# A state-space block with layer norm and tensor-train FFN on eight cores: ten state-sum matmuls issued ahead of the normalisation transposes

## Chip, cores, metric

The kernel runs on all 8 cores of one Trainium2 chip. Each core takes 2 of the 16 sequences and works alone; nothing is exchanged. The metric is the device time of the slowest core in microseconds.

## The reference

x is 16 sequences x 2048 steps x 1024 channels. The output is x plus a selective scan plus a linear layer, both on the normalised x:

```python
xn = _layernorm(x, axis=-1)
x = x + attn(xn) + ffn(xn)
# attn:
x_and_res = x @ in_proj_w.T + in_proj_b
x_in = silu(x_and_res[..., :d_model]); res = x_and_res[..., d_model:]
ssm = x_in @ x_proj_w.T + x_proj_b            # 16 + 1024 + 1024 columns
delta = clip(softplus(ssm[..., :16] @ dt_proj_w.T + dt_proj_b), 1e-5, 0.1)
def step(h, inp):                              # h: batch, 1024, 16
    dt, Bt, Ct, xt = inp
    dA = clip(exp(A * dt[..., None]), 1e-6, 1.0)
    h = clip(h * dA + (Bt * dt * xt)[..., None], -100.0, 100.0)
    return h, sum(h, axis=-1) * Ct + D_param * xt
# scanned over the steps; then y * silu(res) @ out_proj_w.T + out_proj_b
```

The FFN is a 1024 x 1024 matrix built from small tensor-train factors.

## The kernel before

**Work.** The two sequences of a core are cut into 8 chunks of 512 steps (TC). A chunk passes through three stages, and the program goes through windows w = 0 to 9 in which three chunks are in work at once: chunk w-2 has its output projection (cO), chunk w-1 its scan (cS), chunk w its normalisation and projections (cP).

**Scan.** A chunk has 8 channel blocks k of 128 x 16 states n, so 128 scans; scan j is block j // 16, state j % 16. For each, ACT computes a decay plane (emit_da, L899, "da j", ring of DAR = 8 tiles), DVE runs one TENSOR_TENSOR_SCAN over 512 steps (L839, "scan j") into the ring h_buf of HR = 8 slots, and PE adds the plane to a PSUM bank with an identity matmul (emit_sigma, L561, "sum j"). So scan j needs da j and sum j-8 (its slot), and da j needs scan j-8. After four scans DVE clips the carries (L849); half a block after a block's last scan it takes the block's total and makes y (L810, L818), and POOL multiplies by the gate (L458).

**Normalisation.** Each chunk has four tiles t of 128 steps. ACT computes four sums (L957, L962, L967, L973), POOL turns them into mean and variance in six short steps (L433 to L447), ACT takes the reciprocal root (L978, L981), POOL one more step (L450), ACT applies it (L988, or L995 and L999), PE transposes the tile (L628, 8 matmuls into pT1), and ACT copies it out (L1010, L1020) one tile later, after the next tile's apply.

**Output.** Before the normalisation, for each of the four tiles of chunk w-2, PE transposes (L607), ACT copies (L946), POOL loads x again by a DMA of its own queue (L469) and adds (L477), and SP stores.

**What sets the order.** All engines run a list written at build time. BNDS[w] is a table of planned times, one step for each piece of projection work: 8 x 4.32 and 4 x 1.2 us for the output stage (w >= 2 only), 4 x 5.6 for the normalisation tiles, 2.16 for each group of the projections. A scan is planned at SCAN_NS = 1.30 us. On PE, pump() runs ahead of each piece and first issues the sums that are due by then:

```python
if (gn - 3) * SCAN_NS > B:
    break
```

On ACT, apump() does the same for the decay planes, up to 10 us ahead (limit (gn - 6) * SCAN_NS > B + 10) and with a second limit from the sums planned. DVE has no such table; it runs the scans one after the other. For w >= 2 the planned time at the first tile is 39.36 us, then 44.96, 50.56, 56.16, and 61.76 at the first projection group (m = 0). For w = 1 the same five are 0, 5.6, 11.2, 16.8, 22.4. In w = 1 PE also builds the FFN matrix (L542) at m = 0, between the sums and the first projection group.

Of the kernel before, what the change touches and what calls it, by code (L numbers as in the profile page):

```python
# [23 lines left out]
DAR = 8  # L24
DA_HEAD = 16
HR = 8
# [4 lines left out]
SCAN_NS = 1.30  # L31
# [13 lines left out]
def build_core(M_in, M_out):  # L45
# [28 lines left out]
    with es:  # L74
# [79 lines left out]
        def mark(key, chain):  # L154
            M_out[key] = chain.n
# [55 lines left out]
        def c_(tile, i):  # L211
            return tile[:, i:i + 1]
# [299 lines left out]
        def _(te):  # L512
# [35 lines left out]
            for w in range(nch + 2):  # L548
# [3 lines left out]
                sk = [0]  # L552
                bnd = BNDS[w]

                def emit_sigma(gn, cS=cS):
                    k, n = gn // NST, gn % NST
                    sbank = [pS, pS2][k % 2]
                    wt(te, "v", ("scan", cS * 128 + gn))
                    if n == 0 and cS * 8 + k >= 2:
                        wt(te, "v", ("epiy", cS * 8 + k - 2))  # L560
                    TCH(te.matmul(sbank[:, :], eye16[:, :], h_sl(gn),  # L561
                                  start=(n == 0), stop=(n == NST - 1)))
                    mark(("summ", cS * 128 + gn), TCH)

                def pump(_cost=None):
                    B = bnd[sk[0]]
                    sk[0] += 1
                    while sqi[0] < len(sq):
                        gn = sq[sqi[0]]
                        if (gn - 3) * SCAN_NS > B:  # L570
                            break
                        emit_sigma(gn)
                        sqi[0] += 1
# [295 lines left out]
        def _(sc):  # L869
# [12 lines left out]
            for w in range(nch + 2):  # L882
                cO, cS, cP = w - 2, w - 1, w
                dq = list(range(DA_HEAD, 128)) if 0 <= cS < nch else []
                dqi = [0]
                ak = [0]
                bnd = BNDS[w]

                def emit_da(gn, cS=cS):
                    k, n = gn // NST, gn % NST  # L890
                    G = cS * 128 + gn
                    Ps = cS % 2
                    if n == 0:
                        wt(sc, "g", ("u", cS * 8 + k))
                    if G - DAR >= 0:
                        wt(sc, "v", ("scan", G - DAR))
                    if G == 0:
                        wt(sc, "v", ("aclip",))
                    ACH(sc.activation(da_r[gn % DAR][:, :], dlt[Ps][k][:, :],  # L899
                                      AF.Exp, scale=c_(a_cols[k], n)))  # L900
                    mark(("da", G), ACH)

                def _pump_to(B2, B, nom):
                    while dqi[0] < len(dq):
                        gn = dq[dqi[0]]
                        if (gn - nom) * SCAN_NS > B2:
                            break
                        q = gn - DAR
                        req = max(q - HR, 16 * (q // 16) - 1)
                        if req >= 0 and (req - 3) * SCAN_NS > B:  # L910
                            break
                        emit_da(gn)
                        dqi[0] += 1

                def apump(block=False, skip=False):
                    B = bnd[ak[0]]
                    if block:
                        B2 = bnd[min(ak[0] + 3, len(bnd) - 1)] + 10.0
                    else:
                        B2 = B + 10.0  # L920
                    ak[0] += 1
                    if skip:
                        return
                    _pump_to(B2, B, 3 if block else 6)

                def apump_x():
                    B = bnd[max(ak[0] - 1, 0)]
                    _pump_to(B + 10.0, B, 6)

                if cO >= 0:  # L930
                    for m in range(8):
# [16 lines left out]
                if cP < nch:  # L948
                    P = cP % 2
                    for t in range(NTT):  # L950
                        g = cP * NTT + t
                        apump()
                        if t == 0 and cP >= 2:
                            wt(sc, "v", ("epi2", (cP - 2) * 8 + 2))
                            wt(sc, "g", ("u", (cP - 2) * 8 + 2))
                        sc.wait_ge(DS["ldx" + str(g % 2)], (g // 2 + 1) * 16)
                        st1 = ACH(sc.activation(xin[P][2][:, :512],  # L957
                                                x_t[g % 2][:, :512],
                                                AF.Identity,
                                                accum_out=c_(sumx, t)))  # L960
                        sc.wait_ge(ACH.sem, st1)
                        st2 = ACH(sc.activation(xin[P][2][:, :512],  # L962
                                                x_t[g % 2][:, 512:],
                                                AF.Identity,
                                                accum_out=c_(mcol, t)))
                        sc.wait_ge(ACH.sem, st2)
                        st3 = ACH(sc.activation(xin[P][2][:, :512],  # L967
                                                x_t[g % 2][:, :512],
                                                AF.Square,
                                                accum_out=c_(sumsq, t)))  # L970
                        sc.wait_ge(ACH.sem, st3)
                        apump_x()
                        ACH(sc.activation(xin[P][2][:, :512],  # L973
                                          x_t[g % 2][:, 512:], AF.Square,
                                          accum_out=c_(vcol, t)))
                        mark(("stats", g), ACH)
                        wt(sc, "g", ("lnv", g))
                        l0 = ACH(sc.activation(c_(rstd, t), c_(vcol, t), AF.Ln,  # L978
                                               bias=eps_c[:, :]))
                        sc.wait_ge(ACH.sem, l0)  # L980
                        ACH(sc.activation(c_(rstd, t), c_(rstd, t), AF.Exp,  # L981
                                          scale=mhalf_c[:, :]))
                        mark(("rstd", g), ACH)
                        wt(sc, "g", ("nm", g))
                        if g >= 2:
                            wt(sc, "t", ("xntr", g - 2))
                        if t % 2 == 0:
                            ACH(sc.activation(xn_tm[:, :], x_t[g % 2][:, :],  # L988
                                              AF.Identity, bias=c_(nmr, t),
                                              scale=c_(rstd, t)))  # L990
                        else:
                            if t == 1 and cP >= 2:
                                wt(sc, "v", ("epi2", (cP - 2) * 8 + 1))
                                wt(sc, "g", ("u", (cP - 2) * 8 + 1))
                            ACH(sc.activation(xin[P][0][:, :],  # L995
                                              x_t[g % 2][:, :512],
                                              AF.Identity, bias=c_(nmr, t),
                                              scale=c_(rstd, t)))
                            ACH(sc.activation(xin[P][1][:, :],  # L999
                                              x_t[g % 2][:, 512:],  # L1000
                                              AF.Identity, bias=c_(nmr, t),
                                              scale=c_(rstd, t)))
                        mark(("apply", g), ACH)
                        apump_x()
                        if t >= 1:
                            gg = g - 1
                            wt(sc, "t", ("xntr", gg))
                            if cP >= 2 and t == 1:
                                wt(sc, "t", ("outmm", (cP - 2) * 8 + 7))
                            ACH(sc.activation(  # L1010
                                bass.AP(xn_f[P], (t - 1) * 128,
                                        [[DCH * TC, 128], [TC, DCH],
                                         [1, 128]]),
                                bass.AP(pT1, 0,
                                        [[1024, 128], [128, DCH], [1, 128]]),
                                AF.Identity))
                            mark(("xnev", gg), ACH)
# [119 lines left out]
```

## Time and profile before

| | us |
|---|---|
| median of 3 runs (lowest, highest) | 2266.72 (2266.33, 2309.62) |
| the profiled execution | 2282.27 |
| its span on core 7, the slowest | 2280.5 |
| spans of cores 0 to 3 | 2246.6 to 2259.1 |
| spans of cores 4 to 7 | 2268.0 to 2280.5 |
| DVE busy, share of the span | 1606.4 (70%) |
| PE busy | 1280.7 (56%) |
| ACT busy | 1269.6 (56%) |
| POOL busy | 620.9 (27%) |

All times inside the program are from core 7 of the profiled execution, in us from its span's start. A window lasts 228 to 246 us there from w = 2 on. No engine is busy throughout, so the waits have to be read place by place.

### The profile page before, as it was taken

The page shows a single profiled execution, that of the slowest core. Times are in us where ns is not written, and L with a number is a line of the kernel's source. Part 1 is how long each engine was busy: PE and PEld are TensorE (multiplying, and loading weights), DVE is VectorE, ACT ScalarE, POOL GpSimd, SP SyncE. Part 2 cuts the span into 40 slices and gives each one's busy share as a digit, 9 for nine tenths or more (in the row PEclk, how much of TensorE's full clock was granted, in tenths as well). Part 3 has the DMA queues.
Part 4 walks back from the last instruction along what each step waited for, and adds up shares of the span by engine and source line. Part 5 has one row for each costly group of instructions (what it writes and reads, how often), then busy time and mean ns, then how long its engine had stood idle before and what let it go on. Part 6 is the DMA issues. An engine that isn't in the chain of part 4 may idle for free.

```text
span 2280.5 us, 22151 instructions; the slowest of 8 cores (2246.6 to 2280.5 us)
## 1 busy us (share of the span) xinstructions
PE 1280.7 (56%) x5104; PEld 522.6 (23%) x5104; DVE 1606.4 (70%) x1600; ACT 1269.6 (56%) x2001; POOL 620.9 (27%) x570
## 2 busy tenths in 40 slices
PE   1221846366463958196727772776278636855444
PEld 1111312122121313042313221322133212312002
DVE  2332034169975999389958996799679977999980
ACT  0003464566546855586558755875587557845431
POOL 0000041317113071317031713162315231532101
PEclk9999965666575867577858875887588767877557
DMA  5672312630011300231033202220322022302001
GB/s 142 188 177 71 112 59 46 72 60 24 1 65 60 116 19 28 83 98 51 10 102 89 60 10 102 80 69 4 108 77 73 0 93 74 93 1 74 0 10 64
DMA packets 106885, 151.94 MB, mean 67 GB/s; under 512 B 53232, under 2 KB 53240, under 8 KB 106760
## 3 DMA queue, kind: packets, MB, share of 16 engines
q1 hardware_dynamic: 97128, 120.10, 17.7%
q0 software_dynamic: 6176, 19.93, 4.2%
q10 hardware_dynamic: 3456, 10.52, 1.5%
q8 instruction: 46, 0.75, 0.1%
q14 instruction: 79, 0.65, 0.1%
HBM read 124.26 MB, written 26.25 MB: 66 GB/s over the span
## 4 chain that ended last, share of the span: by engine, by line
PE 39%; DVE 21%; issue 12%; ACT 11%; DMA 8%; POOL 6%; SPq 1%; DVEq 0%; ACTq 0%; POOLq 0%
DVE h_buf L839 18%; PE pM L686 7%; PE pS L561 7%; PE pO L589 5%; PE pM L651 5%; PE pO L594 5%; DMA xr_t<-x 4%; PE pO L651 4%; PE pO L686 3%; POOL out_tm L477 3%; ACT da L899 2%; POOL wf L405 1%; PE pT L523 1%; ACT xnf L1010 1%; DMA x_t<-w_x 1%
## 5 line engine op out<-in xcount | busy, mean ns | idle before, releaser
L839 DVE TENSOR_TENSOR_SCAN h_buf<-da,cr,Bu 128x512 f16<-128x512 f16 x768 | 1053.3, 1429 | 181.4 <-PE pS L561 177.4
L899 ACT ACTIVATE da<-dlt,ac 128x512 f16<-128x512 f16 x1024 | 689.6, 715 | 250.8 <-DVE h_buf L839 250.0
L561 PE MATMUL pS<-h_buf,eye 128*128 128x512 f16 x1024 | 427.9, 483 | 317.9 <-DVE h_buf L839 306.0
L839 DVE TENSOR_TENSOR_SCAN h_buf<-da,Bu 128x512 f16<-128x512 f16 x256 | 334.8, 1364 | 180.4 <-ACT da L899 121.8
L458 POOL TENSOR_TENSOR Bu<-y_s,sres 128x512 f16<-128x512 f32 x64 | 125.6, 1962 | 789.8 <-DVE y_s L818 789.8
L561 PEld LDWEIGHTS pS<-h_buf,eye 128*128 128x128 f16 x1024 | 110.1, 109 | 558.5 <-issue 515.9
L686 PE MATMUL pM<-xin,rx 128*128 128x512 f16 (+1 forms) x832 | 209.5, 400 | 16.0 <-ACT sres L1042 14.0
L651 PE MATMUL pM<-xnf,rin 128*128 128x512 f16 x512 | 141.8, 429 | 3.0 <-ACT sres L1042 1.7
L589 PE MATMUL pO<-Bu,wo 128*128 128x512 f16 x512 | 136.8, 415 | 3.1 <-POOL Bu L458 3.1
L651 PE MATMUL pO<-xnf,rin 128*128 128x512 f16 x512 | 130.7, 403 | 4.6 <-DMA rin<-wt_in 4.6
L477 POOL TENSOR_TENSOR out_tm<-otm,xr_t 128x1024 f32<-128x1024 f16 x32 | 74.3, 2321 | 214.5 <-ACT otm L946 112.5
L594 PE MATMUL pO<-xnf,wf 128*128 128x512 f16 x512 | 128.2, 396 | 0.0
L523 PE MATMUL pT<-eye,rx 128*128 128x128 f16 x320 | 40.5, 306 | 142.3 <-DVE rx L736 142.3
L433 POOL TENSOR_TENSOR mcol<-mcol,sumx 128x1 f32<-128x1 f32 x32 | 17.2, 538 | 375.0 <-ACT xin L973 375.0
L686 PEld LDWEIGHTS pM<-xin,rx 128*128 128x128 f16 (+1 forms) x832 | 82.9, 101 | 126.7 <-issue 60.1
L628 PE MATMUL pT<-eye,xn_tm 128*128 128x128 f16 x128 | 16.2, 307 | 165.9 <-ACT xn_tm L988 98.8
L880 ACT ACT_TABLE_LOAD x1 | 1.3, 1283 | 190.4 <-DVE rx L736 190.4
L937 ACT ACTIVATE ao<-pO,bcomb 128x512 f16<-128x512 f32 x64 | 43.9, 685 | 112.5 <-PE pO L594 112.4
L628 PE MATMUL pT<-eye,xin 128*128 128x128 f16 x128 | 16.2, 306 | 153.0 <-ACT xnf L1010 153.0
L946 ACT ACTIVATE otm<-pTo 128x1024 f16<-128x1024 f16 x32 | 32.6, 1020 | 108.4 <-POOL out_tm L477 107.5
L818 DVE SCALAR_TENSOR_TENSOR y_s<-xin,d_cols,y_s 128x512 f32<-128x512 f16 x64 | 49.8, 778 | 59.1 <-POOL Bu L458 52.2
L849 DVE TENSOR_SCALAR cr<-h_buf 128x4 f16<-128x4 f16 x256 | 69.9, 273 | 27.6 <-DVE h_buf L839 0.5
(89 smaller groups left out, 1578.0 us busy)
## 6 DMA issues: line engine op xcount, KB each, us to landing
rin<-wt_in SPq DMA_DIRECT2D x128, 256.0 KB, 2.7
rx<-wt_x SPq DMA_DIRECT2D x128, 256.0 KB, 2.6
x_t<-x SPq DMA_DIRECT2D x32, 512.0 KB, 4.4
xr_t<-x POOLq DMA_DIRECT2D x32, 512.0 KB, 4.6
y<-out_tm SPq DMA_DIRECT2D x32, 512.0 KB, 3.6
wt_in<-rin SPq DMA_DIRECT2D x16, 256.0 KB, 2.9
wt_x<-rin SPq DMA_DIRECT2D x16, 224.0 KB, 3.7
x_t<-w_in ACTq DMA_DIRECT2D x4, 512.0 KB, 4.0
```

Of the source, the lines that this page charges most:

```text
L458: GCH(gp.tensor_mul(Bu[P][k][:, :], y2_s[:, :], sres[P][k][:, :]))
L477: GCH(gp.tensor_add(out_tm[g % 2][:, :], otm16[:, :], xr_t[g % 2][:, :]))
L523: TCH(te.transpose(pT1[:, k * 128:(k + 1) * 128], wst16[j % 2][:, k * 128:(k + 1) * 128], eye16[:, :]))
L561: TCH(te.matmul(sbank[:, :], eye16[:, :], h_sl(gn), start=(n == 0), stop=(n == NST - 1)))
L589: TCH(te.matmul(bank[:, :], w_out[k][:, m * 128:(m + 1) * 128], Bu[P][k][:, :], start=(k == 0), stop=False))
L594: TCH(te.matmul(bank[:, :], w_ffn[k][:, m * 128:(m + 1) * 128], xn_f[P][:, k * TC:(k + 1) * TC], start=False, stop=(k == DCH - 1)))
L651: TCH(te.matmul(bank[:, :], rin[slot][:, k * 128:(k + 1) * 128], xn_f[P][:, k * TC:(k + 1) * TC], start=(k == 0), stop=(k == DCH - 1)))
L686: TCH(te.matmul(out_ap, rx[slot][:, k * ncols:(k + 1) * ncols], xin[P][k][:, :], start=(k == 0), stop=(k == DCH - 1)))
L818: ep2_n[0] = VCH(v.scalar_tensor_tensor(y2_s[:, :], xin[P][kk][:, :], c_(d_cols, kk), y_s[:, :], op0=ALU.mult, op1=ALU.add))
L839: s_n = VCH(v.tensor_tensor_scan(h_sl(gn), da_r[gn % DAR][:, :], Bu[P][k][:, :], init, op0=ALU.mult, op1=ALU.add))
L849: v.tensor_scalar(carry[k][:, n - 3:n + 1], src, 100.0, -100.0, op0=ALU.min, op1=ALU.max))
L899: ACH(sc.activation(da_r[gn % DAR][:, :], dlt[Ps][k][:, :], AF.Exp, scale=c_(a_cols[k], n)))
```

## The change

On PE, the first pump() of the normalisation part (step 12 of the table for w >= 2, step 0 otherwise) may look ahead by the planned length of the four tiles (22.4 us), with a second limit that is the one ACT's decay planes have. On ACT, two extra calls inside the tile loop, apump_x(), are removed, and the helper _pump_to is written back into apump().

```diff
@@ TensorE
+                off_p = 12 if w >= 2 else 0
+
                 def pump(_cost=None):
                     B = bnd[sk[0]]
+                    look = (bnd[min(off_p + 4, len(bnd) - 1)] - B
+                            if sk[0] == off_p else 0.0)
                     sk[0] += 1
                     while sqi[0] < len(sq):
                         gn = sq[sqi[0]]
-                        if (gn - 3) * SCAN_NS > B:
+                        if (gn - 3) * SCAN_NS > B + look:
+                            break
+                        if look > 0 and (gn - 6) * SCAN_NS > B + 10.0:
                             break
                         emit_sigma(gn)
                         sqi[0] += 1
@@ ScalarE
-                def apump_x():
-                    B = bnd[max(ak[0] - 1, 0)]
-                    _pump_to(B + 10.0, B, 6)
...
                         sc.wait_ge(ACH.sem, st3)
-                        apump_x()
                         ACH(sc.activation(xin[P][2][:, :512],
...
                         mark(("apply", g), ACH)
-                        apump_x()
                         if t >= 1:
```

PE's order in window 2, before: the last output transposes (L607), then the sums (L561), the normalisation transposes (L628) of the four tiles, and the first projection group (L651).

```order
L607 MATMUL pTo<-eye16,ao7 128x128
L561 MATMUL pS<-h_buf,eye16 128x512
L628 MATMUL pT1<-eye16,xn_tm 128x128 x8
L561 MATMUL pS<-h_buf,eye16 128x512 x4
L628 MATMUL pT1<-eye16,xin0_0 128x128 x4
L628 MATMUL pT1<-eye16,xin0_1 128x128 x4
L561 MATMUL pS<-h_buf,eye16 128x512 x4
L628 MATMUL pT1<-eye16,xn_tm 128x128 x8
L561 MATMUL pS<-h_buf,eye16 128x512 x5
L628 MATMUL pT1<-eye16,xin0_0 128x128 x4
L628 MATMUL pT1<-eye16,xin0_1 128x128 x4
L561 MATMUL pS<-h_buf,eye16 128x512
```

The same place in the changed kernel, where the transposes have line 634 and the output transposes line 613:

```order
L613 MATMUL pTo<-eye16,ao7 128x128
L561 MATMUL pS<-h_buf,eye16 128x512 x11
L634 MATMUL pT1<-eye16,xn_tm 128x128 x8
L634 MATMUL pT1<-eye16,xin0_0 128x128 x4
L634 MATMUL pT1<-eye16,xin0_1 128x128 x4
L634 MATMUL pT1<-eye16,xn_tm 128x128 x8
L561 MATMUL pS<-h_buf,eye16 128x512 x3
L634 MATMUL pT1<-eye16,xin0_0 128x128 x4
L634 MATMUL pT1<-eye16,xin0_1 128x128 x4
L561 MATMUL pS<-h_buf,eye16 128x512
```

Sum 33 alone stood ahead of the first tile, now sums 33 to 43 do. The four sums ahead of the second and of the third tile are gone, and three of five (44 to 46) are left ahead of the fourth. The last row of each, sum 47, stays at m = 0. Windows 3 to 7 read the same.

PE's order in window 1, before, from the sums ahead of the first tile to the first matmul of the FFN matrix:

```order
L561 MATMUL pS<-h_buf,eye16 128x512 x4
L628 MATMUL pT1<-eye16,xn_tm 128x128 x8
L561 MATMUL pS<-h_buf,eye16 128x512 x4
L628 MATMUL pT1<-eye16,xin1_0 128x128 x4
L628 MATMUL pT1<-eye16,xin1_1 128x128 x4
L561 MATMUL pS<-h_buf,eye16 128x512 x4
L628 MATMUL pT1<-eye16,xn_tm 128x128 x8
L561 MATMUL pS<-h_buf,eye16 128x512 x4
L628 MATMUL pT1<-eye16,xin1_0 128x128 x4
L628 MATMUL pT1<-eye16,xin1_1 128x128 x4
L561 MATMUL pS2<-h_buf,eye16 128x512 x5
L542 MATMUL pO1<-y_s,out_tm0 128x256
```

And in the changed kernel:

```order
L561 MATMUL pS<-h_buf,eye16 128x512 x14
L634 MATMUL pT1<-eye16,xn_tm 128x128 x8
L634 MATMUL pT1<-eye16,xin1_0 128x128 x4
L634 MATMUL pT1<-eye16,xin1_1 128x128 x4
L634 MATMUL pT1<-eye16,xn_tm 128x128 x8
L561 MATMUL pS<-h_buf,eye16 128x512 x2
L634 MATMUL pT1<-eye16,xin1_0 128x128 x4
L634 MATMUL pT1<-eye16,xin1_1 128x128 x4
L561 MATMUL pS2<-h_buf,eye16 128x512 x5
L542 MATMUL pO1<-y_s,out_tm0 128x256
```

Sums 0 to 13 stand ahead of the first tile instead of 0 to 3; sums 14 and 15 come ahead of the fourth, and the five at m = 0 are the same. The rows of ACT, DVE, POOL and SP are the same in both kernels throughout.

## Rows read from the trace of the kernel before

**Rows 1.** Who waited for whom, whole span: total us, times, longest us

```profile
DVE h_buf L839 <- PE pS L561: 232.8, 39, 12.8
...
ACT rstd L978 <- POOL vcol L447: 86.7, 32, 4.2
```

**Rows 2.** Timeline of DVE's scans, window 4, from scan 40: start, length, count

```profile
1153.95 2.69 DVE L839 TENSOR_TENSOR_SCAN h_buf<-da,cr,Bu 128x512 f16<-128x512 f16 x2
...
1169.37 4.30 DVE L839 TENSOR_TENSOR_SCAN h_buf<-da,cr,Bu 128x512 f16<-128x512 f16 x2 [12.73 <-PE pS L561]
...
1183.13 2.46 DVE L839 TENSOR_TENSOR_SCAN h_buf<-da,cr,Bu 128x512 f16<-128x512 f16 x2 [6.12 <-PE pS L561]
...
1194.79 2.46 DVE L839 TENSOR_TENSOR_SCAN h_buf<-da,cr,Bu 128x512 f16<-128x512 f16 x2 [6.46 <-PE pS L561]
...
1209.07 1.28 DVE L839 TENSOR_TENSOR_SCAN h_buf<-da,cr,Bu 128x512 f16<-128x512 f16 x1 [7.90 <-PE pS L561]
```

**Rows 3.** The chain that ended last, in order of time, window 4: start, us, what

```profile
1157.39 2.13 POOL out_tm L477
...
1198.13 0.66 POOL mcol L433
...
1208.38 1.86 PE pS L561 x4
1210.24 3.07 PE pM L651 x8
```

**Rows 4.** Timeline of ACT in window 4: three bursts of decay planes, four reciprocal roots

```profile
1165.22 0.29 ACT L978 ACTIVATE rstd<-vcol,eps_c 128x1 f32<-128x1 f32 x1 [1.55 <-POOL vcol L447]
...
1167.59 3.15 ACT L899 ACTIVATE da<-dlt,ac 128x512 f16<-128x512 f16 x5
...
1177.80 0.29 ACT L978 ACTIVATE rstd<-vcol,eps_c 128x1 f32<-128x1 f32 x1 [4.00 <-POOL vcol L447]
...
1181.34 2.54 ACT L899 ACTIVATE da<-dlt,ac 128x512 f16<-128x512 f16 x4
...
1189.73 0.29 ACT L978 ACTIVATE rstd<-vcol,eps_c 128x1 f32<-128x1 f32 x1 [2.80 <-POOL vcol L447]
...
1193.00 1.93 ACT L899 ACTIVATE da<-dlt,ac 128x512 f16<-128x512 f16 x3
...
1202.21 0.29 ACT L978 ACTIVATE rstd<-vcol,eps_c 128x1 f32<-128x1 f32 x1 [4.23 <-POOL vcol L447]
```

**Rows 5.** Timeline of POOL in window 4, with one scan of DVE beside it

```profile
1164.24 0.22 POOL L438 TENSOR_SCALAR mcol<-mcol 128x1 f32<-128x1 f32 x1
...
1170.44 2.14 POOL L477 TENSOR_TENSOR out_tm<-otm,xr_t 128x1024 f32<-128x1024 f16 x1 [3.27 <-DMA xr_t<-x]
1170.57 3.10 DVE L839 TENSOR_TENSOR_SCAN h_buf<-da,cr,Bu 128x512 f16<-128x512 f16 x1
...
1174.57 0.18 POOL L433 TENSOR_TENSOR mcol<-mcol,sumx 128x1 f32<-128x1 f32 x1
...
1187.08 1.23 POOL L433 TENSOR_TENSOR mcol<-mcol,sumx 128x1 f32<-128x1 f32 x1 [8.16 <-ACT xin L973]
...
1199.94 1.23 POOL L438 TENSOR_SCALAR mcol<-mcol 128x1 f32<-128x1 f32 x1
```

**Rows 6.** POOL's output add in all windows (shortest, median, longest ns), and one of window 6

```profile
L477 POOL TENSOR_TENSOR out_tm<-otm,xr_t x32: 2119/2145/3012, 664.1 to 2272.6; 128x1024 f32<-128x1024 f16 x32
...
1612.62 2.96 POOL L477 TENSOR_TENSOR out_tm<-otm,xr_t 128x1024 f32<-128x1024 f16 x1 [4.61 <-DMA xr_t<-x]
```

**Rows 7.** Timeline of window 1, first tile: DVE, POOL and ACT

```profile
320.55 4.57 DVE L839 TENSOR_TENSOR_SCAN h_buf<-da,Bu 128x512 f16<-128x512 f16 x4
...
325.33 0.21 POOL L438 TENSOR_SCALAR mcol<-mcol 128x1 f32<-128x1 f32 x1
...
326.31 0.29 ACT L978 ACTIVATE rstd<-vcol,eps_c 128x1 f32<-128x1 f32 x1 [2.17 <-POOL vcol L447]
...
335.95 0.29 ACT L978 ACTIVATE rstd<-vcol,eps_c 128x1 f32<-128x1 f32 x1 [2.91 <-POOL vcol L447]
```

More of the change, by code:

```diff
@@ L901, in emit_da @@
                     mark(("da", G), ACH)
[L903 to L913, printed above, removed]
                 def apump(block=False, skip=False):
@@ L923, in apump @@
                         return
-                    _pump_to(B2, B, 3 if block else 6)
-                def apump_x():
-                    B = bnd[max(ak[0] - 1, 0)]
-                    _pump_to(B + 10.0, B, 6)
+                    while dqi[0] < len(dq):
+                        gn = dq[dqi[0]]
+                        if True:
+                            if (gn - (3 if block else 6)) * SCAN_NS > B2:
+                                break
+                            q = gn - DAR
+                            req = max(q - HR, 16 * (q // 16) - 1)
+                            if req >= 0 and (req - 3) * SCAN_NS > B:
+                                break
+                        emit_da(gn)
+                        dqi[0] += 1
                 if cO >= 0:
```

## The prediction

> **What bounds the kernel now.** I read the list of who waited for whom first. DVE, the busiest engine, waits 232.8 us for PE's state sums in 39 waits, the longest 12.8 us [rows 1]. The timeline of DVE then says where: in window 4 scans 40 and 41 run at 1153.95, and after them come four waits of 12.73, 6.12, 6.46 and 7.90 us, each ended by a sum [rows 2]. That is 33.2 us, and seven windows of that size make 232: all of this wait lies in the normalisation part. Its cause is the order: sum 34 stands behind the first tile's transposes, and these wait for ACT's apply.
>
> The question is whether those waits set the end. The chain in order of time, read through the same stretch, says no: it runs over POOL's add, then over ACT's and POOL's steps of the four tiles, and reaches PE with the sums at 1208.38 and the first projection group at 1210.24 [rows 3]. DVE is not on it. So the part lasts as long as the tiles' own chain lasts, and DVE waits because it is faster than that chain. The last of its waits, ended at 1209.07, is scan 55 waiting for sum 47, which stands at m = 0, behind the fourth tile's copy.
>
> **What moves.** On PE ten sums per window, 34 to 43 in windows 2 to 7 and 4 to 13 in window 1, go ahead of the first tile. Sum 47 (window 1: sums 16 to 20) stays at m = 0. Hence scan 55 starts, as before, when the four tiles are through. This is the step on which all else rests: scans before it can run early, but nothing after it can start earlier unless the tiles' chain itself gets shorter. The direct gain is 0.
>
> The removed ACT calls cost and give nothing: apump_x() uses the step that apump() has just used, with the same two limits, so it never had anything to issue, and ACT's order is the same row for row.
>
> Does the first tile now wait on PE? Sum 43 needs scan 43. Scan 41 ends at 1156.64 (1153.95 + 2.69), scans 42 and 43 need 2 x 1.26 us and perhaps 1.9 us of POOL's add between them, so sum 43 is done by about 1162. The transposes wait for the apply anyway, which ends just before the da burst, about 1167.6. Cost 0, with 5 us of cover; past that it would be paid one for one, with the transposes, the copy and all projections queued behind it.
>
> **What changes in the tiles' chain.** It holds six short POOL steps per tile, and these are slow when a scan runs. Step L438 takes 0.22 us with DVE idle and 1.23 us at 1199.94, and L433 1.23 us at 1187.08, both in a burst of scans; the other way round a scan beside POOL's add takes 3.10 us instead of 1.26 [rows 5]. ACT's wait for the variance shows the price: 1.55 us with DVE idle, 4.00, 2.80 and 4.23 us in the next three tiles of window 4 [rows 4]. Over all 32 tiles it is 86.7 us [rows 1]; at 1.5 each 48 would be left, so 38.7 us is the most that moving scans out of the way can ever give here.
>
> The Trainium skill, "SBUF — State Buffer", on the door between DVE and GpSimd, says that the pair of ports they share is an exclusive lock: a DVE instruction with two SBUF inputs and a GpSimd one that reads SBUF never overlap, and the later one blocks fully. The trace agrees, 0.22 against 1.23 us, with one short step let through per scan. By that rule early scans are not free where POOL is on the chain, which speaks against this change at two places below.
>
> Now the bursts, in window 4. After the change a burst starts when its da is there (0.75 us after ACT's burst begins) and no more 1.79 us after it (1194.79 against 1193.00) [rows 2, 4].
>
> - Before the first tile: scans 42 and 43 fall on POOL's add at 1157.39, which is on the chain. It can wait for the rest of a scan: 2.96 us has been seen for a median of 2.145 [rows 6], so 0 to 0.84. I take +0.3, since about half the windows have the add start in DVE's gap.
> - Second tile: five scans (44 to 48) instead of four, starting 1.04 us earlier, beside POOL's add (1170.44), the gate and the steps from 1174.57 on [rows 5]. The burst ends 1.26 - 1.04 = 0.2 us later at least, and the add can lose 0.4 to a running scan, and so can the gate. Bounds +0.2 and +1.5; I take +0.9.
> - Third tile: scans 49 to 51 only, from 1182.1 to about 1186, since scan 52 needs sum 44. POOL's first step at 1187.08 finds DVE idle: 2.80 - 1.55 = -1.2. Bounds -1.25 and 0.
> - Fourth tile: scans 52 to 54 start with sum 44 at the old time, 1194.8, and end at 1198.6 where five scans ended at 1201.2. POOL begins at 1198.13 [rows 3] and loses 0.4 instead of 4.23 - 1.55 = 2.7: -2.3. Bounds -2.7 and -1.0.
>
> Sum for a window from 2 to 7: 0.3 + 0.9 - 1.2 - 2.3 = -2.3 us, six times -13.8.
>
> Window 1 goes the other way. There scans 8 to 11 end at 325.1 and DVE stops, and POOL's first-tile steps pass, L438 in 0.21 us [rows 7]. Now scans 12 to 15 follow at once, 4 x 1.14 us, to about 330.1, over all the remaining steps. Each of three or four steps waits about 1.05 us: +3.5 (bounds 0 and 4 x 1.05 = 4.2). The second tile has only scans 16 and 17, done before POOL's steps: 2.91 - 1.5 = -1.4. Net +2.1.
>
> Total: -13.8 + 2.1 = -11.7 us. After the fourth tile every queue reads as before, so this shift goes through to the end. The profiled execution took 2282.3 us, 15.6 more than the median of the runs shown; it would become 2270.6, and the median 2266.7 - 11.7 = 2255.0.
>
> Its own range: with the three costs at their best (0 for the add, +0.2, window 1 at 0) it gains 6 x (0.3 + 0.7) + 3.5 = 9.5 more, 2245.5. With them at their worst and the third tile's gain lost it is 6 x (0.5 + 0.6 + 1.2) + 0.7 = 14.5 less, 2269.5.
>
> **Rivals.** A. The early scans pay directly. If something else than sum 47 held scan 55, DVE would keep its lead: 2 x 1.26 for scans 42 and 43 and 1.04 for each of two bursts, 4.6 us a window, 6 x 4.6 = 28, and some 7 in window 1: 2267 - 35 = 2232. For it speaks that DVE is the busiest engine and loses 232.8 us here; against it, the place of sum 47 and a chain without DVE. Chance 0.10.
>
> B. The port decides the other way: slower. Scans 42 and 43 run late enough to lie on POOL's first-tile steps. The point is scan 43 ending after about 1164, where those steps begin [rows 5]; in window 4 there are 2 to 3 us to spare. Price: 2 x 1.05 there, the full 0.84 on the add, 1.5 on the second tile and, as a load issued by POOL lands later when scans run (wait 4.61 against 3.27 us [rows 5, 6]), up to 1.3 more. That is 2.1 + 0.84 + 1.5 + 1.3 = 5.7 against 3.5 gained, +2.2 x 6 + 4.2 = 17: 2284. Chance 0.17.
>
> C. No net effect: POOL's steps meet as many scans as before, at other tiles. DVE's waits change their names and the part keeps its length: 2267, give or take 5. Chance 0.18.
>
> D. That the limit does not let the sums through is excluded by the order.
>
> The forecast keeps 0.55. Its own range holds most of that and of C; reaching to part of A and B gives 2238 to 2281. Two per cent, about what a measurement of this kernel can tell from no change, is 45 us, more than the 38.7 us that could be gained and far more than B's 17. I give 0.03 to faster, 0.93 to within, 0.04 to slower.
>
> **What would show it.** DVE's wait for the sums should fall from 232.8 to about 110 us and its wait for da planes rise by about 80, with a wait for da 44 and da 49 in each window; if scan 55 starts noticeably before the four tiles are through, the argument is wrong at its root. ACT's wait for the variance should fall from 86.7 to about 75: near 5 us at the second tile, 1.6 at the third, 2.0 at the fourth, and 5 to 6 at the first of window 1. If it stays at 86.7, C holds; if it rises, B. The chain should still pass through POOL's steps, and the transposes of the first tile should wait for the apply, not for a sum.

## The result, and the profile after

| | before | after |
|---|---|---|
| median, us (lowest to highest, 10 runs each, same chip) | 2270.39 (2263.2 to 2309.62) | 2250.11 (2244.44 to 2252.8) |
| DVE's wait for the sums, all windows | 232.8 | 105.4 |
| ACT's wait for the variance, all tiles | 86.7 | 68.9 |
| span, median of cores 0 to 3 | 2257.4 | 2244.7 |
| the same, counted from the end of window 0's normalisation | 2036.0 | 2018.8 |

The ratio is 0.9914, interval 0.9899 to 0.9929, so the change takes off 19.5 us, 16 to 23; that is clear of the noise and under 1%. The forecast was 11.7 off; sign and range hold, the size is too small by 8. Where a median and a ratio below don't fit each other, it is because the ratios leave out runs in which one half of the chip had a lower granted clock, which happens to every kernel here.

The last line of the table removes something that has nothing to do with the change: window 0's normalisation ends anywhere from 218.7 to 232.0 us, over both kernels and all cores. The stage itself takes 33.8 us on every core; what differs is its start, and with it how long DVE has waited for its first loads until then (62.1 to 75.6 us on the eight cores before). From there on cores 0 to 3 are 17.2 us faster, and that is the number which the parts below must add up to.

Busy times say little of it. The first part of the page of the kernel after, to be held against the table ahead of the prediction (DVE 1606.4, PE 1280.7, ACT 1269.6, POOL 620.9):

```profile
PE 1243.4 (55%) x5104; PEld 511.5 (23%) x5104; DVE 1620.5 (72%) x1600; ACT 1269.8 (56%) x2001; POOL 606.0 (27%) x570
```

The list of who waited for whom, of the kernel after (core 1; total us, times, longest), answers to [rows 1]:

```profile
DVE h_buf L845 <- ACT da L905: 118.5, 7, 110.3
DVE h_buf L845 <- PE pS L561: 105.4, 15, 8.3
DVE h_buf L845 <- PE pT L634: 79.9, 14, 7.9
ACT rstd L977 <- POOL vcol L447: 68.9, 32, 4.8
```

The two waits in the table are core 7's before and core 1's after; on core 0, where the granted clocks were 0.750 and 0.754, they went from 219.1 to 106.8 us and from 86.6 to 68.6.

DVE's wait for the sums fell by 127.4 us and the time by 19.5: the largest change in the profile is not the gain. Of the 127.4, 79.9 us have only changed their name and stand in the third row. (The first row is not new: DVE waited 122.0 us for planes before.) Another 14.1 us have become busy time of DVE, 1606.4 to 1620.5 with 1600 instructions in both, since more scans now lie beside POOL's add and gate: the first four of the burst below take 7.50 us, where four take 4.81 in the rows of e7 further down. The fourth row fell from 86.7 to 68.9, by 17.8, and this small one is where the gain is.

DVE's scans in window 4 of the kernel after, from scan 40, answer to [rows 2]. Start, length, count, and in brackets the idle time before:

```profile
1132.10 6.63 DVE L845 TENSOR_TENSOR_SCAN h_buf<-da,cr,Bu 128x512 f16<-128x512 f16 x4
...
1146.60 7.50 DVE L845 TENSOR_TENSOR_SCAN h_buf<-da,cr,Bu 128x512 f16<-128x512 f16 x4 [7.60 <-PE pT L634]
...
1154.38 1.32 DVE L845 TENSOR_TENSOR_SCAN h_buf<-da,cr,Bu 128x512 f16<-128x512 f16 x1
...
1160.53 3.63 DVE L845 TENSOR_TENSOR_SCAN h_buf<-da,cr,Bu 128x512 f16<-128x512 f16 x3 [4.84 <-PE pT L634]
...
1172.07 3.63 DVE L845 TENSOR_TENSOR_SCAN h_buf<-da,cr,Bu 128x512 f16<-128x512 f16 x3 [7.62 <-PE pS L561]
...
1183.95 1.28 DVE L845 TENSOR_TENSOR_SCAN h_buf<-da,cr,Bu 128x512 f16<-128x512 f16 x1 [8.25 <-PE pS L561]
```

DVE still stops four times. Scans 42 and 43 now join 40 and 41, the next burst has five scans, then three and three, and scan 55, the last row, still waits until the tiles are through. The idle time in the brackets is 28.3 us where it was 33.2.

ACT's work in the same window, with the first tile's transposes on PE, answers to [rows 4]:

```profile
1138.66 0.62 ACT L957 ACTIVATE xin<-x_t 128x512 f16<-128x512 f32 x1
...
1143.37 0.29 ACT L977 ACTIVATE rstd<-vcol,eps_c 128x1 f32<-128x1 f32 x1 [1.55 <-POOL vcol L447]
...
1145.73 3.15 ACT L905 ACTIVATE da<-dlt,ac 128x512 f16<-128x512 f16 x5
1145.96 1.01 PE L634 MATMUL pT<-eye,xn_tm 128*128 128x128 f16 x8 [6.71 <-ACT xn_tm L987]
...
1156.11 0.29 ACT L977 ACTIVATE rstd<-vcol,eps_c 128x1 f32<-128x1 f32 x1 [4.18 <-POOL vcol L447]
...
1167.01 0.29 ACT L977 ACTIVATE rstd<-vcol,eps_c 128x1 f32<-128x1 f32 x1 [1.76 <-POOL vcol L447]
...
1177.10 0.29 ACT L977 ACTIVATE rstd<-vcol,eps_c 128x1 f32<-128x1 f32 x1 [1.83 <-POOL vcol L447]
...
1181.99 1.02 ACT L1018 ACTIVATE xnf<-pT 128x1024 f16<-128x1024 f16 x1 [1.25 <-PE pT L634]
```

The four waits were 1.55, 4.00, 2.80 and 4.23 us and are 1.55, 4.18, 1.76 and 1.83. The second tile is where it was, a little longer; the third and the fourth no longer wait for blocked POOL steps. From the first row's start to the last one's end is the normalisation part, 44.35 us. It is the measure used from here on, since cores differ in it by 0.3 us or less in most windows (0.7 at most) while a span scatters. In us, windows 1 to 7, core 0:

| | w1 | w2 | w3 | w4 | w5 | w6 | w7 | sum |
|---|---|---|---|---|---|---|---|---|
| before | 42.8 | 47.0 | 47.1 | 47.6 | 46.7 | 47.1 | 47.0 | 325.3 |
| after | 43.6 | 43.8 | 44.1 | 44.3 | 44.0 | 43.8 | 43.8 | 307.4 |

The difference is 17.9 us, beside 17.2 from end to end. The time went out of the normalisation part; what lies between two parts did not get shorter (933.6 us before and 936.7 after, five stretches on core 0).

POOL in window 4 after the change shows how, to be read against [rows 5]:

```profile
1152.98 1.10 POOL L433 TENSOR_TENSOR mcol<-mcol,sumx 128x1 f32<-128x1 f32 x1
1154.05 0.18 POOL L435 TENSOR_TENSOR vcol<-vcol,sumsq 128x1 f32<-128x1 f32 x1
...
1154.62 1.07 POOL L444 TENSOR_TENSOR nmr<-mcol 128x1 f32<-128x1 f32 x1
...
1165.40 0.19 POOL L433 TENSOR_TENSOR mcol<-mcol,sumx 128x1 f32<-128x1 f32 x1 [8.17 <-ACT xin L972]
...
1175.41 0.27 POOL L433 TENSOR_TENSOR mcol<-mcol,sumx 128x1 f32<-128x1 f32 x1 [7.28 <-ACT xin L972]
```

In the second tile two steps take 1.1 us, one for each scan they meet. DVE's burst has a gap of 0.28 us between its fourth scan (which ends at 1154.10) and the next at 1154.38, in which it clips the carries, and L435 to L441, 0.6 us together, get through around it. In the third tile DVE runs no scan (1164.16 to 1172.07) and in the fourth it is just finishing one (1175.70), and a step takes 0.2 to 0.3.

### The profile page after: what moved, and what is told of

Its sections match the earlier page's. It is cut to its first block, busy times and chain, and to the rows that moved or that the text cites. A ratio compares the mean times of both kernels' runs of the same rounds, so it can differ in the third digit from the quotient of the medians.

```text
span 2251.1 us, 22151 instructions; the slowest of 8 cores (2229.5 to 2251.1 us)
## 1 busy us (share of the span) xinstructions
PE 1243.4 (55%) x5104; PEld 511.5 (23%) x5104; DVE 1620.5 (72%) x1600; ACT 1269.8 (56%) x2001; POOL 606.0 (27%) x570
## 4 chain that ended last, share of the span: by engine, by line
PE 37%; DVE 23%; issue 11%; ACT 11%; DMA 9%; POOL 7%; SPq 1%; DVEq 0%; ACTq 0%; POOLq 0%
DVE h_buf L845 20%; PE pM L692 7%; PE pS L561 7%; PE pM L657 5%; PE pO L595 5%; DMA xr_t<-x 4%; PE pO L600 4%; PE pO L657 4%; POOL out_tm L477 3%; PE pO L692 3%; ACT da L905 2%; POOL wf L405 1%; PE pT L523 1%; ACT xnf L1008 1%; DMA x_t<-w_x 1%
## 5 line engine op out<-in xcount | busy, mean ns | idle before, releaser
L845 DVE TENSOR_TENSOR_SCAN h_buf<-da,cr,Bu 128x512 f16<-128x512 f16 x768 | 1071.5, 1454 | 140.5 <-PE pS L561 77.4
L561 PE MATMUL pS<-h_buf,eye 128*128 128x512 f16 x1024 | 421.7, 471 | 359.1 <-DVE h_buf L845 349.2
L561 PEld LDWEIGHTS pS<-h_buf,eye 128*128 128x128 f16 x1024 | 107.3, 105 | 608.8 <-issue 547.3
L692 PE MATMUL pM<-xin,rx 128*128 128x512 f16 (+1 forms) x832 | 198.3, 384 | 22.9 <-ACT sres L1040 19.1
L477 POOL TENSOR_TENSOR out_tm<-otm,xr_t 128x1024 f32<-128x1024 f16 x32 | 81.0, 2533 | 204.6 <-ACT otm L946 103.7
L657 PE MATMUL pM<-xnf,rin 128*128 128x512 f16 x512 | 133.5, 409 | 3.9 <-ACT sres L1040 2.5
L595 PE MATMUL pO<-Bu,wo 128*128 128x512 f16 x512 | 131.9, 404 | 3.1 <-POOL Bu L458 3.1
L657 PE MATMUL pO<-xnf,rin 128*128 128x512 f16 x512 | 123.3, 386 | 8.4 <-DMA rin<-wt_in 8.4
L433 POOL TENSOR_TENSOR mcol<-mcol,sumx 128x1 f32<-128x1 f32 x32 | 11.7, 364 | 371.6 <-ACT xin L972 371.6
L937 ACT ACTIVATE ao<-pO,bcomb 128x512 f16<-128x512 f32 x64 | 43.8, 685 | 99.6 <-PE pO L600 99.6
L946 ACT ACTIVATE otm<-pTo 128x1024 f16<-128x1024 f16 x32 | 32.6, 1020 | 111.6 <-POOL out_tm L477 110.7
L692 PE MATMUL pO<-xin,rx 128*128 128x512 f16 x256 | 74.5, 444 | 16.4 <-ACT dlt L1086 16.4
```

Of the source, the lines that this page charges most:

```text
L477: GCH(gp.tensor_add(out_tm[g % 2][:, :], otm16[:, :], xr_t[g % 2][:, :]))
L561: TCH(te.matmul(sbank[:, :], eye16[:, :], h_sl(gn), start=(n == 0), stop=(n == NST - 1)))
L595: TCH(te.matmul(bank[:, :], w_out[k][:, m * 128:(m + 1) * 128], Bu[P][k][:, :], start=(k == 0), stop=False))
L657: TCH(te.matmul(bank[:, :], rin[slot][:, k * 128:(k + 1) * 128], xn_f[P][:, k * TC:(k + 1) * TC], start=(k == 0), stop=(k == DCH - 1)))
L692: TCH(te.matmul(out_ap, rx[slot][:, k * ncols:(k + 1) * ncols], xin[P][k][:, :], start=(k == 0), stop=(k == DCH - 1)))
L845: s_n = VCH(v.tensor_tensor_scan(h_sl(gn), da_r[gn % DAR][:, :], Bu[P][k][:, :], init, op0=ALU.mult, op1=ALU.add))
```

## The experiments

The theory of the forecast, called P below: the tiles' chain over ACT and POOL paces the part, and the change only moves scans away from POOL's short steps. Its rivals: A, the early scans pay directly (the expectations call it L), and C, nothing changes but the names of waits. A cut in an edit is marked by three dots. Each ratio is against runs of the kernel before on the same chip.

### Taking POOL's short steps off the chain: e2 and e3

This is the run that can kill P. If POOL's steps are computed on ACT, no scan can block them, and the ten moved sums must be worth nothing. ACT computes the same values. e2 starts from the kernel before, e3 from the kernel after:

```diff
-                        s1 = GCH(gp.tensor_add(c_(mcol, t), c_(mcol, t),
-                                               c_(sumx, t)))
...
-                        wt(sc, "g", ("lnv", g))
+                        sc.wait_ge(ACH.sem, ACH.n)
+                        q1 = ACH(sc.activation(c_(mcol, t), c_(mcol, t),
+                                               AF.Identity,
+                                               bias=c_(sumx, t)))
...
+                        q3 = ACH(sc.activation(c_(nmr, t), c_(mcol, t),
+                                               AF.Square,
+                                               scale=1.0 / 32.0))
```

e2, expected:

> The kernel before, with POOL's short steps of the normalisation done by ACT instead (six steps of about 0.3 us, of which ACT waits out each one's end). No GpSimd step is left in the tile from the sums to the apply. Theory P: the 38.7 us that POOL's steps lost behind scans go away, and a little of the fixed waits too; 2270 - 38 = 2232, give or take 8; the normalisation part of windows 2 to 7 has one length in all tiles, about 40 us instead of 47. Theory L: the tiles' chain was not what set the time; DVE's waits for the sums stay, and the gain is below 15 us.

e3, expected:

> The changed kernel with the same move to ACT. Theory P: with no POOL step in the tile the ten sums issued early have nothing left to give, so this one and e2_before_act differ by less than 5 us, and this one may be the slower one, since scans 42 and 43 lie on POOL's output add. Theory L: the ten sums give their 20 us here as well, and this one is 15 to 20 us faster than e2_before_act.

e2 measured 2220.87 us, ratio 0.9776 (0.9751 to 0.9801); e3 measured 2221.99, ratio 0.9796 (0.9773 to 0.9818). The parts sum to 276.2 us in both. DVE's waits in e2, then in e3:

```profile
DVE h_buf L812 <- PE pS L534: 186.5, 36, 12.4
```

```profile
DVE h_buf L818 <- PE pS L534: 100.6, 17, 7.7
DVE h_buf L818 <- PE pT L607: 74.5, 13, 7.2
```

This pair settles it. The move of the ten sums does the same to DVE's waits as before, 186.5 to 100.6, and gives nothing once POOL is off the chain; if anything e3 is a little slower, within the intervals. A is out for this change. And the steps themselves were worth 49.1 us in the parts. That is more than the 38.7 of the forecast, which is what scans add to the variance wait, and e2 ended 3 us below the range given for it (2224 to 2240). Moving the steps also saves ACT's wait for L450, 17.0 us in the list of the kernel before, and replaces the 1.5 us that every tile pays with DVE idle by ACT's own steps; how the surplus divides between the two was not measured.

The Trainium skill, "SBUF — State Buffer", in its section "Summary: rules for kernel authors", says of a DVE instruction with two SBUF inputs and a GpSimd one that reads SBUF that the second to issue blocks fully, and advises: "Schedule whichever is off the critical path". The runs agree on the cost (L433 takes 1.10 us beside a scan and 0.19 without), and show another way that is worth more here: take the GpSimd side off the path altogether, 50.8 us (e2, 2.24% of 2269.0) against the 19.5 of moving scans.

### The same sums behind the first tile: e4

```diff
-                    look = (bnd[min(off_p + 4, len(bnd) - 1)] - B
-                            if sk[0] == off_p else 0.0)
+                    B0 = bnd[min(off_p, len(bnd) - 1)]
+                    look = 22.4 if sk[0] == off_p + 1 else 0.0
```

> The changed kernel with the same ten sums issued behind the first tile's transposes instead of ahead of them (in window 1 too). The sums that run early are the same, and the ones left for the third and fourth tile too. Theory P: scans 42 to 48 now come in one burst of seven on the second tile; ACT's wait there rises from 4.2 to about 6 us, and stays at 1.5 in the third and fourth; in window 1 the first tile goes back to 2.2 and the second rises to 5. Six times 2 us: 2260, give or take 4. Theory L: the same early sums give the same gain, 2250.

2265.89 us, ratio 0.9985 (0.9966 to 1.0004), 2 us above the range of P (2256 to 2264) and far from the 2250 of A. The parts sum to 320.4, 4.9 less than before and 13.0 more than after, where P had said 12. Reciprocal roots of the second and third tile in window 4:

```profile
1160.20 0.29 ACT L977 ACTIVATE rstd<-vcol,eps_c 128x1 f32<-128x1 f32 x1 [6.00 <-POOL vcol L447]
...
1171.20 0.29 ACT L977 ACTIVATE rstd<-vcol,eps_c 128x1 f32<-128x1 f32 x1 [1.76 <-POOL vcol L447]
```

Third and fourth tile are as good as in the kernel after (1.76 here, 1.76 there). But scans 42 and 43, which the kernel after runs before any tile's steps begin, now fall into the second tile's burst with all the others, and it waits 6.00 us. In window 1 the first tile waits 2.17 us and the second 4.68, as P had it. The position of the sums matters by what scans meet, tile by tile.

### Window 1 by itself: e1 and e8

e1 is the kernel after with the look-ahead only for w >= 2, e8 only for w == 1:

```diff
-                            if sk[0] == off_p else 0.0)
+                            if sk[0] == off_p and w >= 2 else 0.0)
```

> Theory P (POOL's short steps on the tiles' chain meet fewer scans; scans run early pay nothing by themselves): the look-ahead is taken away in window 1 alone. ACT's wait for the variance goes back from 4.79 to 2.2 us at that window's first tile and from 1.5 to 2.9 at its second, the normalisation part of window 1 is 42.9 us instead of 43.6, and the whole gains nothing or about 1 us on the changed kernel: 2249 to 2250, ratio to before 0.991. Theory L (DVE's lead pays directly): window 1 gives back its seventh of the gain, 3 us, or more, as four scans ran early there instead of two: 2253 to 2254.

> The look-ahead in window 1 alone. Theory P: its normalisation part grows from 42.8 to 43.6 us and nothing else moves: no change that can be measured against the kernel before, 2268 to 2271. Theory L: four scans run early there, 3 to 4 us less. The run without window 1 was 5 us slower than the changed kernel; if that was more than scatter, this one is 5 to 6 us faster than before.

e1: 2255.4 us, ratio 0.9941 (0.9919 to 0.9962). e8: 2272.61, ratio 0.9993 (0.9963 to 1.0023). In the parts both do what P says: window 1 is 42.8 us long without the change and 43.6 with it, whatever the other windows do. In the times neither can show 0.8 us. Taken alone, e1's 2255.4 fits A (2253 to 2254) better than P (2249 to 2250); but its interval overlaps that of the kernel after, and e8, where A has 3 to 4 us less than before, shows no gain. What window 1 costs in the end stays open at the size of a microsecond or two.

In window 1 after the change the first tile reads, against [rows 7]:

```profile
321.31 4.57 DVE L845 TENSOR_TENSOR_SCAN h_buf<-da,Bu 128x512 f16<-128x512 f16 x4
321.42 1.12 POOL L441 TENSOR_SCALAR vcol<-vcol 128x1 f32<-128x1 f32 x1
322.50 1.14 POOL L444 TENSOR_TENSOR nmr<-mcol 128x1 f32<-128x1 f32 x1
...
324.84 0.29 ACT L977 ACTIVATE rstd<-vcol,eps_c 128x1 f32<-128x1 f32 x1 [4.79 <-POOL vcol L447]
...
333.05 0.29 ACT L977 ACTIVATE rstd<-vcol,eps_c 128x1 f32<-128x1 f32 x1 [1.47 <-POOL vcol L447]
```

### Freeing scan 55: e5 and e6

The forecast rested on sum 47, which stays behind the tiles. e5 is the kernel after with sums up to 50 ahead of the fourth tile; ACT's planes stay:

```diff
-                            if sk[0] == off_p else 0.0)
+                            if sk[0] == off_p else
+                            5.6 if sk[0] == off_p + 3 and w >= 2 else 0.0)
```

> The changed kernel with sums 47 to 50 issued ahead of the fourth tile's transposes too (windows 2 to 7), so that scan 55, its clip and the block's y (1.28 + 0.17 + 0.69 + 0.75 = 2.9 us of DVE) are no longer held until the four tiles are through. Theory P alone (only the tiles' chain counts): the fourth tile's burst has four scans instead of three, POOL's steps there lose another 1 to 2 us, six times: 2256 to 2262. Theory P with a DVE bound after the tiles (the rest of a window is paced by the scans, so a lead that survives the tiles pays in full): 2.9 us less and 1.2 more per window, about -10: 2240.

2256.99 us, as P alone had it (2256 to 2262); ratio 0.9947 (0.9914 to 0.9979), some 7 us above the kernel after. The intervals overlap a little, but the parts agree, 313.4 us together against 307.4. Its waits:

```profile
DVE h_buf L846 <- ACT da L906: 168.5, 16, 115.1
...
ACT rstd L978 <- POOL vcol L447: 74.9, 32, 4.8
```

The wait for sums fell again, to 60.4 us, and that for planes rose from 118.5 to 168.5: scan 55 starts earlier, and the scans behind it wait for planes that ACT's table holds back. The fourth tile pays for it, 2.54 us for its variance instead of 1.55, since a scan is back at its steps.

e6 moves both, sums and planes, by lists of last indices for the four tiles, with POOL's steps still on POOL:

```diff
+                    if w >= 2 and 1 <= sk[0] - 1 - off_p <= 3:
+                        lim = (43, 47, 51, 54)[sk[0] - 1 - off_p]
+                        while sqi[0] < len(sq) and sq[sqi[0]] <= lim:
+                            emit_sigma(sq[sqi[0]])
...
+                        adx((43, 50, 56, 61)[ak[0] - 1 - 12])
...
+                            adx((45, 52, 58, 63)[t])
```

> The changed kernel with the scans let through the whole normalisation part of windows 2 to 7: sums 44 to 54 stand ahead of the second, third and fourth tile's transposes, and ACT issues decay planes up to 63 there (two behind each tile's sums, where it waits for POOL, and the rest in the bursts) instead of up to 55. No work is added. If only the tiles' chain counts: eight more scans beside POOL's steps, 2 to 4 us more per window, 2262 to 2275. If a lead that survives the tiles pays: eight scans and the block's y are 8 x 1.45 + 1.4 = 13 us a window, six times 78, less some 20 for POOL's steps and 10 for ACT's longer bursts: about 2200.

2293.51 us, ratio 1.0083 (1.0055 to 1.0112): slower than before, and worse than both theories had it. The part is 51 us, 7 more than in the kernel after, where 2 to 4 had been expected, and the sum of the parts, 350.2 us against 307.4, covers the whole loss of 43 against the kernel after. ACT computes 8 more planes in it (5 us, by the 3.15 for five in [rows 4]), and POOL's steps meet more scans (ACT's wait for the variance is 81.7 us, although the last line of the edit now puts two planes per tile into that wait). DVE has no use of it: in window 4 it stands for 15.14 us, waiting for a sum that PE's table holds back:

```profile
1215.00 1.28 DVE L851 TENSOR_TENSOR_SCAN h_buf<-da,cr,Bu 128x512 f16<-128x512 f16 x1 [15.14 <-PE pS L561]
```

### A lead on DVE with POOL off the chain: e7, e9, e10

By how much DVE's scans run ahead of their planned times is called its lead. e7 is e3 with such lists (sums 43, 47, 51, 56; planes 43, 50, 56, 63).

> e3_after_act (steps on ACT) with the same lead: sums 44 to 56 ahead of the later tiles, decay planes up to 63 in three bursts of 7, 6 and 7 instead of 5, 4 and 3. POOL's steps are not in the tile, so the scans collide with nothing on the chain. If only the tiles' chain counts: eight planes of 0.63 us more on ACT there, 5 us a window: 2222 + 30 = 2252. If the lead pays: 78 less and 30 more, about 2175 to 2180, the fastest of all.

2242.64 us, ratio 0.9859 (0.9818 to 0.9899): worse than e3 by 20.7 us in the medians and by 14 in the ratios, where a lead had been expected to pay. Core 0's scans in window 4:

```profile
1156.78 4.81 DVE L824 TENSOR_TENSOR_SCAN h_buf<-da,cr,Bu 128x512 f16<-128x512 f16 x4
...
1179.49 4.81 DVE L824 TENSOR_TENSOR_SCAN h_buf<-da,cr,Bu 128x512 f16<-128x512 f16 x4 [17.63 <-ACT da L884]
```

DVE gets through scan 63 inside the part, where the kernel after gets to 54, and then stands for 17.63 us, waiting for plane 64. The part grew by 5 us with the planes (the seven sum to 305.3 us against 276.2), and behind it the two tables of planned times hold sums and planes to the old schedule, so most of the lead is given back. What was left to show is that the tables do this. e9 is e7 with the tables 10.4 us further behind the part (eight scans at 1.30), on PE and on ACT:

```diff
                     B = bnd[sk[0]]
+                    if w >= 2 and sk[0] >= off_p + 4:
+                        B += 10.4
...
                     B = bnd[ak[0]]
+                    if w >= 2 and ak[0] >= 16:
+                        B += 10.4
```

> e7_lead_act let eight more scans through the tiles and was 20 us slower than e3_after_act; in its trace DVE then stands 17.6 us idle in window 4 for decay plane 64, which the table holds back until the fifth projection group. Here the table is moved with it: behind the tiles PE's sums and ACT's planes are issued 10.4 us (eight planned scans) further ahead. Theory K (a lead pays if the table carries it on, because the scans pace the rest of the window): 8 x 1.45 + 1.4 = 13 us a window off, 5 us of planes in the tiles on, from 2222: 2175, give or take 10, and the 17.6 us wait is gone. Theory P alone (nothing but the tiles' own chain counts anywhere): 2250, as e7_lead_act.

e10 is the same with half the lead (sums to 54, planes to 59, 5.2 us):

> The same with half the lead: decay planes up to 59, sums up to 54, the table 5.2 us ahead behind the tiles. Theory K: 4 x 1.45 + 1.4 = 7 us a window off and 2.5 on: 2222 - 27 = 2195. Theory P alone: 2222 + 15 = 2237.

e9: ratio 0.9596 (0.9551 to 0.9642), 92 us below the kernel before (median of all runs 2200.97, the profiled one 2180.74). e10: 0.9711 (0.9666 to 0.9756), 2214.52. The wait of 17.63 us behind the part has shrunk to 5.36 in e9 (core 0, window 4), and its profiled run lies in the range of theory K (2175, give or take 10), which adds to P that the scans pace the rest of a window; e10 lies between K (2195) and P alone (2237). Both beat the two kernels of this study; e9 is 4% faster than before and 3.2% faster than after (0.9596 / 0.9914 = 0.968). The stretch from the end of one normalisation part to the start of the next, core 0, in the kernel after, in e7 and in e9 (us; PE, PEld, DVE, ACT and POOL busy, each with its count; granted clock, DMA share, GB/s):

```profile
1180.00:1367.00 187.00, 137.27 (x557) 55.21 (x555) 179.69 (x163) 123.59 (x186) 62.48 (x37) 0.81 0.21 65
```

```profile
1166.00:1350.00 184.00, 135.92 (x547) 54.72 (x547) 164.46 (x149) 118.42 (x177) 58.81 (x36) 0.80 0.22 65
```

```profile
1145.00:1322.00 177.00, 131.96 (x547) 54.29 (x546) 165.59 (x149) 118.43 (x178) 59.32 (x37) 0.83 0.23 69
```

In the kernel after DVE is busy 179.69 of 187 us, so the scans nearly fill the stretch. e7 takes 15 us of scans out of it, 164.46, and it stays 184 long, since the tables hold it. e9 has the same work in it and is 177 long. The part itself is 44.4 in both. What no run separates is the moved tables without a lead: the stretch of the kernel after, with its 179.69 us of DVE's work, could not be 177 long, but some of the gain may come from the tables alone.

## Why the forecast was right, and where it was off

**Direct gain 0, by sum 47.** Right, and shown by e2 and e3. Scan 55 starts at 1183.95, 8.25 us after DVE stopped and just after the last copy's end at 1183.01; the chain in that stretch of the kernel after still runs over POOL's steps and reaches PE with the sums:

```profile
1152.98 1.10 POOL mcol L433
1154.62 1.08 POOL nmr L444
...
1175.41 0.27 POOL mcol L433
...
1183.26 1.86 PE pS L561 x4
1185.12 2.78 PE pM L657 x8
```

But the reason was too narrow: by the prediction, all after scan 55 hangs on sum 47, so freeing it should start the later ones. e5 freed it and lost 7 us: ACT's table still held the planes of the next scans. Sums, planes and the tables behind the tiles all have to move; e9, which also has POOL's steps on ACT, is the run in which they do.

**apump_x() is empty.** ACT's order is unchanged; no run was made on it alone.

**First tile not delayed.** Right: its transposes waited 6.71 us for the apply, not for a sum, and its variance wait is 1.55 in both kernels in windows 2 to 7.

**The four terms of a window 2 to 7**, by ACT's wait for the variance and the parts, means of the six windows on core 0:

| term | forecast | measured |
|---|---|---|
| output add | +0.3 | +0.5 to +0.7 |
| second tile | +0.9 | +0.2 (4.01 to 4.17) |
| third tile | -1.2 | -1.0 (2.51 to 1.53) |
| fourth tile | -2.3 | -2.3 (3.94 to 1.64) |
| the part (the three tiles), from its lengths | -2.6 | -3.1 |

The output add is read from the stretch between ACT's first output copy (L946) and the start of the part, which grew by 3.0 to 4.4 us on cores 0 to 3, over six windows; scans 42 and 43 do lie on it. The add's median, with the 2145 ns of [rows 6] before, is now (core 7 there, core 1 here; on core 0 it went from 2180 to 2686)

```profile
L477 POOL TENSOR_TENSOR out_tm<-otm,xr_t x32: 2120/2521/3165, 657.9 to 2243.1; 128x1024 f32<-128x1024 f16 x32
```

The term that was mis-sized is the second tile's. It was priced as the burst's extra length plus losses of add and gate, 0.4 us each. In window 4 the add did lose 0.4 (2.54 us for 2.14), but the gate nothing (2.06 in both). And the burst's length does not count, since POOL waits by the step: two of its steps were blocked before (L435 and L438, 1.09 and 1.24 us) and two are blocked after (1.10 and 1.07), because the clip between two scans lets steps pass. After the change the fourth scan blocks one step and the fifth, behind the clip, one more; the first three are over before the steps begin. Six times 0.7 are 4.2 us.

**Window 1.** Forecast +3.5 for the first tile and -1.4 for the second, together +2.1; measured +2.6 (2.17 to 4.79) and -1.44 (2.91 to 1.47), and the part is 0.8 longer. Three steps were blocked (1.12, 1.14 and, for L447, 0.97 us) for 0.9 each, where three to four at 1.05 were taken. The fourth tile gained another 0.4, a term that the forecast left out: 1.3 us in all.

**The sum.** In the parts 17.9 us were gained, and 11.7 + 6 x 0.3 = 13.5 were forecast for them, so 4.4 are missing. By the waits they are 4.2 for the second tile, 1.3 for window 1 and -1.2 for the third tile, 4.3 in all. The output add went the other way: it cost 3.0 to 4.4 us where 1.8 were forecast, so part of the forecast's sum was right by two errors of opposite sign. From the parts' 17.9, less that, one would get 13.5 to 15 us from end to end; 17.2 were seen on cores 0 to 3 and 19.5 (16 to 23) in the runs of the slowest core. What is between may be scatter such as window 0's; it was not followed up, and stays open.

**What would show it.** DVE's wait for sums, about 110: 105.4. ACT's wait for the variance, about 75: 68.9, lower by 6, the second tile again. The wait for planes, up by about 80: under that name it didn't move (122.0 before, 118.5 after); it stands under PE's transposes, see the last section.

**Rivals.** A is excluded by e2 and e3 and by scan 55. B needed scan 43 at the first tile's steps; they show 1.55 us in windows 2 to 7, so it did not happen there, though in window 1 and in e4 the port does just what B says. C is excluded by 17.2 us from end to end; e4 is what it would have looked like.

## What to carry to other kernels

Ask which engine's chain lasts in a stretch, not which engine idles there: here 127 us of the busiest engine's waits left their row of the list for a gain of 19.5 us, and ACT's 87 us of waits for steps of one column were the lever. A GpSimd step of one column took 1.1 us beside a scan and 0.2 without, so look for such steps on the chain; if the engine that needs their result can compute them, give them to it (e2). And when an order is held by tables of planned times, a lead gained in one place is worth little until the tables behind it are moved with it (e7 and e9 have the same lists: 14 to 20 us slower than e3 with the old tables, over 40 faster with the moved ones).

## What had not been expected of the hardware

- DVE's new wait for planes 44 and 49 is listed under PE's transposes (79.9 us in 14 waits). The plane is the only one of the two that scan 44 needs: ACT's burst begins at 1145.73 and its first plane is due 0.72 us later, at 1146.45, the scan starts at 1146.60, and the transposes ran from 1145.96 on beside it. A releaser in such a list is the last event that fits, and is worth checking against what the instruction reads.
- Three short steps of POOL can pass while DVE clips the carries: L435 to L441 took 0.6 us around a gap of 0.28 us, where one step takes 1.1 when it meets a scan. So the number of blocked steps depends not only on the number of scans but on where the clip after every fourth of them falls. That this is why five scans cost a tile hardly more than four had is read from window 4's rows; no run moved the clip.
- A core's first normalisation ended anywhere from 218.7 to 232.0 us. That scatter of 13.3 us is two thirds of the whole effect, and it goes into the time of the slowest core.
